# Making one-hot columns eight at a time and adding four experts with TensorE

## The reference, cut to what matters

```python
x = x + windowed_attention(layernorm(x))               # stage 1
t = x.reshape(16 * 2048, 128)
# graph attention over 524288 random edges and 32768 self loops (stage 2)
h = (layernorm(t) @ W_gat).reshape(M, 4, 4)
e = leaky_relu(a_src[src] + a_dst[dst], 0.2)
alpha = exp(e - segment_max(e, dst)[dst]) / segment_sum(...)
agg = segment_sum(h[src] * alpha, dst)
# the last stage (stage 3)
scores = layernorm(agg + b_gat).reshape(M, 4 heads, 4 experts).mean(1)
w = softmax(top_k(scores, 2))                          # zero for the two experts not chosen
out = t + sum_e w[e] * (gelu(x @ W1[e] + b1[e]) @ W2[e] + b2[e])
```

## Time and profile before

| What | Value |
|---|---|
| Time, median of 3 executions | 11302.15 us (11301.26 to 11305.25) |
| The profiled execution's own time | 11406.52 us |
| Its span, first to last instruction | 11404.8 us |
| Busy share of the span | DVE 47%, POOL 43%, PE 37%, PEld 20%, ACT 19% |
| Granted TensorE clock, mean | 0.629 |
| `attention` | until about 1976 us |
| `edges` | about 1976 to 10824.6 us |
| `combine` | 10824.6 to 11404.8 us |
| Transfers of `combine` for each image | 2048 KB of expert outputs, 512 KB of tokens, 512 KB of results |

### The profile page before, as it was taken

One profiled execution on the slowest core, in us unless ns is written; L12 is line 12 of the kernel. 1 busy time (PEld: TensorE's weight loads), 2 busy tenths in 40 slices (PEclk: granted clock), 3 DMA queues, 4 the chain that ended last, 5 costly groups with the idle time before them and its releaser, 6 DMA issues. The chain is left out here.

```text
span 11404.8 us, 104675 instructions
## 1 busy us (share of the span) xinstructions
PE 4230.9 (37%) x31385; PEld 2300.7 (20%) x31448; DVE 5397.3 (47%) x14623; ACT 2169.7 (19%) x4631; POOL 4862.3 (43%) x5600
## 2 busy tenths in 40 slices
PE   6899987223222222222222223322222222222300
PEld 4666665011111111111111111111111111111100
DVE  9999998233333333333333333333333333333437
ACT  5777775000000000000000000000000000000015
POOL 3222221644444444444444444444444444444261
PEclk8999998555555555555555555555555555555555
DMA  1222222000001110100000000000110100010147
GB/s 51 59 59 59 59 59 64 16 22 22 22 22 25 27 22 22 22 22 22 22 22 22 22 22 22 22 22 22 29 23 22 22 22 22 22 22 22 32 136 220
DMA packets 503856, 419.15 MB, mean 37 GB/s; under 512 B 160546, under 2 KB 400338, under 8 KB 502866
## 3 DMA queue, kind: packets, MB, share of 16 engines
q1 hardware_dynamic: 355842, 356.89, 9.9%
q0 software_dynamic: 147552, 56.96, 4.3%
HBM read 203.44 MB, written 176.45 MB: 33 GB/s over the span
## 5 line engine op out<-in xcount | busy, mean ns | idle before, releaser
L1602 POOL DMA_INDIRECT edge_G<-node_rows,edge_src x4352 | 4113.1, 945 | 4601.1 <-DVEq L1359 3293.7
L1651 PE MATMUL edge_cbank<-edge_ohh,edge_ohl 128*128 128x256 bf16 x4096 | 1481.1, 396 | 6159.5 <-DVE edge_ohh L1419 5207.8
L1419 DVE TENSOR_SCALAR edge_ohh<-edge_iob,edge_dlf 128x256 bf16<-128x256 bf16 x4096 | 1220.1, 300 | 2169.1 <-issue 2168.9
L1418 DVE TENSOR_SCALAR edge_ohl<-edge_iob,edge_dlf 128x128 bf16<-128x128 bf16 x4096 | 1107.5, 271 | 2159.5 <-issue 2114.5
L1651 PEld LDWEIGHTS edge_cbank<-edge_ohh,edge_ohl 128*128 128x128 bf16 x4096 | 434.4, 106 | 7199.7 <-DVE edge_ohh L1419 5948.5
L1627 ACT ACTIVATE edge_hid<-edge_hbank,edge_b1c 128x512 f32<-128x512 f32 x512 | 351.7, 687 | 7228.5 <-PE edge_hbank L1658 7199.7
L1431 DVE TENSOR_TENSOR edge_yo<-edge_ybank,edge_b2r 128x512 f32<-128x512 f32 x256 | 177.0, 692 | 1003.5 <-PE edge_ybank L1667 940.1
L569 POOL TENSOR_TENSOR attn_nw<-attn_st 128x8 f32<-128x8 f32 x64 | 42.4, 662 | 1409.6 <-DVE attn_st L1024 1409.6
L1658 PE MATMUL edge_hbank<-edge_xt,edge_w 128*128 128x512 f32 x1024 | 601.4, 738 | 29.2 <-ACT edge_hid L1627 16.3
L1667 PE MATMUL edge_ybank<-edge_w,edge_hid 128*128 128x128 f32 x4096 | 477.7, 278 | 76.3 <-ACT edge_hid L1627 62.0
L1667 PEld LDWEIGHTS edge_ybank<-edge_w,edge_hid 128*128 128x128 f32 x4096 | 465.7, 193 | 130.0 <-issue 100.6
(11 more groups left out here) (268 smaller groups left out, 6001.4 us busy)
## 6 DMA issues: line engine op xcount, KB each, us to landing
edge_G<-node_rows,edge_src POOLq DMA_INDIRECT x4352
expert_out<-edge_yo SPq DMA_DIRECT2D x64, 1024.0 KB
comb_ye<-expert_out SPq DMA_DIRECT2D x32, 2048.0 KB
state_rows<-edge_O SPq DMA_DIRECT2D x64, 816.0 KB, 3.6
attn_km<-attn_kT SPq DMA_DIRECT2D x1024, 32.0 KB, 2.0
attn_xin<-in_x SPq DMA_DIRECT2D x32, 512.0 KB, 4.4
attn_xres<-in_x SPq DMA_DIRECT2D x32, 512.0 KB, 5.4
x_rows<-attn_x SPq DMA_DIRECT2D x32, 512.0 KB, 3.4
```

The lines of the kernel that those rows point to most:

```text
L1418: dve.tensor_scalar(ohl[:, t % RING, :], iob[:, 0:P], dlf[:, 0, t:t + 1], None, ALU.is_equal)
L1419: dve.tensor_scalar(ohh[:, t % RING, :], iob[:, :], dlf[:, 1, t:t + 1], None, ALU.is_equal).then_inc(s_oh, 1)
L1602: pool.indirect_dma_start(G[b][:, t, :], None, node_rows, bass.IndirectOffsetOnAxis(ap=src[b][:, t:t + 1], axis=0)).then_inc(s_g[b][2 * t ...
L1651: pe.matmul(cbank[b][:, 0:HI], ohl[:, t % RING, :], ohh[:, t % RING, :], start=(t == 0), stop=(t == HC - 1)).then_inc(s_ohp, 1)
```

## The change

In `edges`, DVE makes the one-hot tiles of eight columns with two instructions in place of sixteen. Each is a `tensor_tensor` comparison of the column numbers, repeated eight times, with eight destinations, each repeated over the width. The ring grows from 8 to 16 slots, so two batches of eight fit. DVE waits until PE has used a whole batch of slots, and PE waits once for each eight columns. PE's matmuls stay as they are, one for each column.

In `combine`, one DVE instruction weighs all four experts of an image in place (4096 elements for each partition). PE adds the four parts by multiplying each half of each part with the identity, accumulating in PSUM: eight float32 matmuls of 512 columns for each image. DVE adds the tokens and writes the result. ACT keeps only the gates' exponential. The ranking of experts takes nine instructions in place of eighteen, and the batches are 4, 8, 8, 6, 4 and 2 images.

```diff
-RING = 8
+WIDE = 8
+RING = 2 * WIDE
@@ counts, DVE
-                for t in range(HC):
+                for t in range(0, HC, WIDE):
                     if t >= RING or not first_of(b, i):
-                        dve.wait_ge(s_ohp, c * HC + t - RING + 1)
-                    dve.tensor_scalar(ohl[:, t % RING, :], iob[:, 0:P], dlf[:, 0, t:t + 1], None, ALU.is_equal)
-                    dve.tensor_scalar(ohh[:, t % RING, :], iob[:, :], dlf[:, 1, t:t + 1], None, ALU.is_equal).then_inc(s_oh, 1)
+                        dve.wait_ge(s_ohp, c * HC + t + WIDE - RING)
+                    r = t % RING
+                    dve.tensor_tensor(ohl[:, r:r + WIDE, :], iob[:, 0:P].unsqueeze(1).to_broadcast([P, WIDE, P]),
+                                      dlf[:, 0, t:t + WIDE].unsqueeze(2).to_broadcast([P, WIDE, P]), ALU.is_equal)
+                    dve.tensor_tensor(ohh[:, r:r + WIDE, :], iob[:, :].unsqueeze(1).to_broadcast([P, WIDE, HI]),
+                                      dlf[:, 1, t:t + WIDE].unsqueeze(2).to_broadcast([P, WIDE, HI]), ALU.is_equal).then_inc(s_oh, 1)
@@ counts, PE
                 for t in range(HC):
-                    pe.wait_ge(s_oh, c * HC + t + 1)
+                    if t % WIDE == 0:
+                        pe.wait_ge(s_oh, c * (HC // WIDE) + t // WIDE + 1)
                     pe.matmul(cbank[b][:, 0:HI], ohl[:, t % RING, :], ohh[:, t % RING, :],
                               start=(t == 0), stop=(t == HC - 1)).then_inc(s_ohp, 1)
@@ combine
-    SIZES = (8, 8, 8, 8)
+    SIZES = (4, 8, 8, 6, 4, 2)
@@ combine, ACT: weigh() and its calls are gone
@@ combine, PE
+            for m in range(IMAGES):
+                b = m % BUFS
+                if m >= 2:
+                    pe.wait_ge(s_res, m - 1)
+                pe.wait_ge(s_scaled, m + 1)
+                for h in range(2):
+                    for x in range(EXPERTS):
+                        last = pe.matmul(total[m % 2][:, h * BANK:(h + 1) * BANK], ident[:, :],
+                                         ye[b][:, h * TILES // 2:(h + 1) * TILES // 2, x * P:(x + 1) * P],
+                                         start=x == 0, stop=x == EXPERTS - 1)
+                last.then_inc(s_total, 1)
@@ combine, DVE: ranking
-                for u in range(EXPERTS):
-                    for v in range(u + 1, EXPERTS):
-                        (three instructions on one pair of experts)
+                for d in range(1, EXPERTS):
+                    (the same three on all pairs that lie d apart)
@@ combine, DVE: for each image
+            def weigh(k, m):
+                ...
+                dve.tensor_tensor(parts, parts, gate[:, at:at + TILES, :].unsqueeze(3).to_broadcast([P, TILES, EXPERTS, P]),
+                                  ALU.mult).then_inc(s_scaled, 1)
+            def result(m):
+                ...
+                dve.wait_ge(s_total, m + 1)
+                dve.tensor_tensor(res[b][:, :, :], total[m % 2][:, :].rearrange("p (t d) -> p t d", d=P), xr[b][:, :, :],
+                                  ALU.add).then_inc(s_res, 1)
             for k in range(BATCHES):
                 gates(k)
                 for m in range(FIRST[k], FIRST[k] + SIZES[k]):
+                    weigh(k, m)
+                    if m > FIRST[k]:
+                        result(m - 1)
+                result(m)
```

More of the change, by code:

```diff
@@ L1696, in combine @@
     assert sum(SIZES) == IMAGES
-    def by_vector(m):
-        return 2 - m % 2
     with ExitStack() as ctx:
@@ L1722, in combine @@
         sc = sb("sc", [P, BT, EXPERTS])
-        beat = sb("beat", [P, BT])
+        beat = sb("beat", [P, BT, EXPERTS - 1])
+        ident = sb("ident", [P, P])
+        total = [ctx.enter_context(nc.psum_tensor(f"comb_total{i}", [P, TILES * P], F32)) for i in range(2)]
         rank = sb("rank", [P, BT, EXPERTS])
@@ L1736, in combine @@
         s_scaled = sem("s_scaled")
+        s_ident = sem("s_ident")
+        s_total = sem("s_total")
         s_res = sem("s_res")
@@ L1764, in _ @@
         def _(act):
[L1765 to L1774, removed]
             for k in range(BATCHES):
@@ L1780, in _ @@
                 act.activation(gate[:, 0:tiles, :], gate[:, 0:tiles, :], ACT.Exp).then_inc(s_ex, 1)
-                act.wait_ge(s_gate, k + 1)
-                for m in range(FIRST[k], FIRST[k] + SIZES[k]):
-                    weigh(k, m)
+        @block.tensor
+        def _(pe):
+            pe.wait_ge(s_ident, 2)
+            for m in range(IMAGES):
[9 more added lines that the diff above has]
+                last.then_inc(s_total, 1)
         @block.gpsimd
         def _(pool):
+            pool.memset(ident[:, :], 0.0).then_inc(s_ident, 1)
+            pool.wait_ge(s_ident, 1)
+            pool.affine_select(out=ident[:, :], in_=ident[:, :], compare_op=ALU.not_equal, fill=1.0,
+                               base=0, pattern=[[-1, P]], channel_multiplier=1).then_inc(s_ident, 1)
             for k in range(BATCHES):
@@ L1847, in gates @@
                 link(dve.tensor_reduce(mx[:, 0:N], sc[:, 0:N, :], AX_X, ALU.max))
-                for u in range(EXPERTS):
-                    for v in range(u + 1, EXPERTS):
[L1850 to L1853, removed]
+                for d in range(1, EXPERTS):
+                    won = beat[:, 0:N, 0:EXPERTS - d]
+                    link(dve.tensor_tensor(won, sc[:, 0:N, 0:EXPERTS - d], sc[:, 0:N, d:EXPERTS], ALU.is_ge))
+                    link(dve.tensor_tensor(rank[:, 0:N, d:EXPERTS], rank[:, 0:N, d:EXPERTS], won, ALU.add))
+                    link(dve.scalar_tensor_tensor(out=rank[:, 0:N, 0:EXPERTS - d], in0=rank[:, 0:N, 0:EXPERTS - d], scalar=1.0, in1=won,
+                                                  op0=ALU.add, op1=ALU.subtract))
                 link(dve.tensor_scalar(rank[:, 0:N, :], rank[:, 0:N, :], 2.0, None, ALU.is_lt))
@@ L1862, in gates @@
                 dve.sem_inc(s_gate, 1)
+            def weigh(k, m):
+                b = m % BUFS
+                dve.wait_ge(s_ye[b], 16 * (m // BUFS) + 16)
+                at = (m - FIRST[k]) * TILES
+                parts = ye[b][:, :, :].rearrange("p t (x d) -> p t x d", d=P)
+                dve.tensor_tensor(parts, parts, gate[:, at:at + TILES, :].unsqueeze(3).to_broadcast([P, TILES, EXPERTS, P]),
+                                  ALU.mult).then_inc(s_scaled, 1)
+            def result(m):
+                b = m % BUFS
+                dve.wait_ge(s_xr[b], 16 * (m // BUFS) + 16)
+                if m >= BUFS:
+                    dve.wait_ge(s_st[b], 16 * (m // BUFS))
+                dve.wait_ge(s_total, m + 1)
+                dve.tensor_tensor(res[b][:, :, :], total[m % 2][:, :].rearrange("p (t d) -> p t d", d=P), xr[b][:, :, :],
+                                  ALU.add).then_inc(s_res, 1)
             for k in range(BATCHES):
```

## The result

| Kernel | Median | Against the kernel before |
|---|---|---|
| before | 11301.7 us (11286.9 to 11305.3) | 1 |
| after | 10843.4 us (10835.7 to 10855.7) | 0.9596, interval 0.9581 to 0.9611 |

The change takes 458 us off, 4.0%. I had forecast 11460 us, slower. The measured time lies in the stated range (10780 to 11750 us) but on the other side of the kernel before.

A forecast was written before the change was run, and what follows sets the result against it. Bound: engines held to one instruction per 1.40 us while gathers are worked off. Profiled 11406.5 + 126 (edge stage) + 37 (last stage) = 11570 us; median 104 us lower, 11466, say 11460 us; range 10780 to 11750.

The forecast's parts named there:

- slow stretch: Edge stage, each chunk: engines pass about one instruction per 1.40 us, until 95.2 us after the chunk's first gather.
- while gathers are worked off: All engines: the condition under which each passes about one instruction per 1.40 us once a burst is used up.
- so at the onset (G + 6.5) about 8 columns are seen as used: Counting: 6.5 us after a chunk's first gather (G) slowing starts; 33 more columns follow, 41 to 42 in all.
- E + 6.7: Edge stage: `hist` 6.7 us after the slow instruction pace ends (E), against 4.9 before; +1.8 us a chunk, +2.0 with clock.
- slower still: Rival, chance 0.18: batch 6 misses the slow pace's end, +5.2 us a chunk, last stage +110 us: 11740 us.
- loads not counted: Rival, chance 0.20: PE's loads escape the spacing, a column costs 1.40 us, `hist` 15 us earlier, -8.5 x 62: 10810 us.
- 68 x 1.40 us: Edge stage: slow pace lasts 95.2 us from the first gather, set by a chunk's 68 gathers, unchanged.
- Batch 7 gets in: Rival, chance 0.12: 48 columns seen before the slow pace ends, so the last batch fits, -3.4 us a chunk: 11125 us.
- DVE alone is held: Rival, chance 0.08: only DVE's one-hot `tensor_scalar` is slowed beside POOL, a chunk takes 95.2 us: 8650 us.
- +37: Last stage: predicted change in us, 617 against 580.2, with images 44 us apart while gathers run; bounds -20 to +110.

The follow-up runs named there:

- held_before: The kernel before, with POOL also waiting for a chunk's counts before beginning its gathers, so none runs beside counting: 11594.2 us, 1.025.
- keys_psum: The kernel after, with a chunk's 128 decoded destinations in PSUM, so one-hot instructions read one operand from SBUF: 10961.9 us, 0.9686.
- held_after: The kernel after, with POOL also waiting for the chunk's counts before beginning the next gathers: 11780.1 us, 1.0339.
- math_first: The kernel after, with DVE's order counts, `math`, outputs in place of counts, outputs, `math` (but for the last chunk): 9977.6 us, 0.873.
- combine_only: The kernel before with only the last stage's part of the change, edge stage as before: 11244.8 us, 0.9936.
- edges_only: The kernel after with the last stage of the kernel before, so only the edge part of the change: 10915.0 us, 0.9647.

## Why the prediction was wrong

**What bounds the edge stage: right in the main.** The slow stretch comes with the gathers and hits all engines (`held_before`). With gathers of 0.94 us it lasts 95.2 to 95.6 us from the first gather, in the kernels before, `keys_psum`, `held_before` and `held_after`. It ends 10 to 12 us after POOL's last issue in before, after, `keys_psum` and `math_first`, and PE's loads count (2.80 us a column, 44 us for an output tile; I had taken 2.66). An instruction each 1.40 us was the right reading. My words "while gathers are worked off" say too much: in the kernel before nothing is transferred from 5176 to 5184 us, while the stretch lasts until 5183.1.

```profile
DMA packets 0, 0.00 MB, mean 0 GB/s; under 512 B 0, under 2 KB 0, under 8 KB 0
```

**The step that failed** is "so at the onset (G + 6.5) about 8 columns are seen as used". G + 6.5 was where DVE had passed 37 instructions at full pace, and I took it for a moment that holds for all engines. It is not: in `keys_psum` PE passes some 60 instructions first, and 32 columns are seen at G + 19.7. From there 27 more fit into the stretch at 2.8 us, so 59 of 64 and not 42 are seen before its end, the last batch is built 34 us ahead of it, and PE has long done the five that are left when they become seen: `hist` at E + 0.2 in place of E + 6.7, and 4.7 us a chunk won where I had 2.0 lost. No row of the kernel before shows PE's count, since PE waited there for DVE's next column throughout; I should have kept a range for this term and not one value. With the measured 2.80 us a column in place of 2.66, my own sum would also have had 40 columns at E, at the edge of the rival "slower still". (In "loads not counted" 8.5 us went by 62 chunks where all other terms go by 63, 9 us of difference.)

Whether each engine has a burst of its own isn't settled. One shared by all would nearly fit these two kernels too: 37 instructions of DVE and about 30 of PE before, 10 of DVE and about 60 of PE in `keys_psum`. In the last stage of before, DVE is spaced when ACT passes its 23 at full pace, which speaks against it, but DVE itself passes eight at that moment:

```profile
10961.94 0.42 DVE L1861 TENSOR_TENSOR comb_gate<-comb_gate,comb_mx 128x256 f32<-128x256 f32 x1 [0.85 <-issue]
10962.85 2.22 DVE L1878 SCALAR_TENSOR_TENSOR comb_res<-comb_ye,comb_gate,comb_xr 128x128 f32<-128x128 f32 x8 [0.48 <-DVE comb_gate L1861]
```

Nor is the count a fixed one: DVE passed 37 in the edge stage of before and 31 in the gates of its first batch. Either way the step fails: the onset is no fixed time after the first gather.

**What I left out** is that the new instructions stretch POOL's gathers. With it `hist` comes at G + 28.8 and the spacing sets in only after counting. In the chunk read above the end of the slow stretch is 15.4 us later, and 22.4 us are gone behind it. How much of this is the stretching's own is seen on one chip: a chunk takes 136.4 us with the old counting (`combine_only`), 131.7 with the new one and free gathers (`keys_psum`), and 130.0 with stretched gathers (`edges_only`). So 4.7 us come without the stretching and 1.7 us with it, some 100 us in the medians. I had put the end of the stretch at 68 x 1.40 us from the first gather, whatever DVE does. With eight gathers done by the end of counting at G + 26.9, the other 60 at 1.40 us each give G + 110.9, and G + 110.6 was measured. The Trainium skill has the rule, "SBUF — State Buffer", section "Who interferes with whom": a VectorE instruction with two SBUF inputs contends with a GpSimd instruction that reads SBUF. The trace agrees: a gather, which reads its indices `edge_src` from SBUF, takes 3.03 us with two SBUF inputs on DVE and 0.94 with one of them in PSUM.

**The rivals.** "Loads not counted" gave 10810 us, 33 us from the result, and is false: loads count, and `hist` is 71 us ahead of its old place, not 15. A right number was no evidence for it. "Batch 7 gets in" gave 11125 us and is, as a mechanism, what the edge stage of `keys_psum` does, with a term of -3.4 us a chunk where 4.7 was measured. "DVE alone is held" is refuted by `held_before`: the same `tensor_scalar` runs at full pace without gathers, and the later output tiles wait for PE.

**The last part.** The durations were right (4.4 us weighing, 1.2 us the sum) or a little high (6.9 us an image at full pace for 7.65). What was wrong is the place of the spacing: I had four images at up to 44 us in the first batch, the kernel after has none there. Where they do occur, the stage takes 604 us against my 617. So +37 was -72, and why the spacing stays away from the first batch the runs didn't settle.

## What to carry to other kernels

A stall that sets in after 6 us in one kernel may set in much later in another, where another engine does the work; look for the longest run at full pace of every engine before giving it a time, and where no row shows it, put a range. When a change replaces one-input instructions by two-input ones on VectorE, look at what GpSimd issues beside them. And ask what stands behind the end of a bound that can't be moved: the change itself took off 4%, and moving `math` under the gathers another 8%. Where chips differ, compare a change only with kernels run on the same chip.

## What was unexpected of the hardware

- A gather issued beside DVE's `tensor_tensor` with two SBUF operands took 3.03 us (4.02 beside the 4.4 us weighing), and 0.94 us when one operand lay in PSUM.
- That delay made the kernel faster, about 100 us: eight gathers in 27 us leave the other engines at full pace.
- PE passed about 60 instructions, loads included, before the 1.40 us spacing reached it (`keys_psum`), ACT 23 (last stage of before), DVE 37, 31 or 21 by stage and kernel, and in the first gates of the kernel after it passed all 46. What the spacing is made of no run shows.
- The spacing outlasts the gathers' transfers: none is recorded in the last 7 us of the slow stretch of before.
